# One run of transposes for x and h in the feed-forwards of a three-part transformer block

## What is computed

```python
def ffn(x, w_gate, w_up, w_down):          # fp4_linear rounds both operands to FP4 in blocks of 16
    gate = fp4_linear(x, w_gate)            # 256 -> 704
    y = fp4_linear(x, w_up)
    return fp4_linear(silu(gate) * y, w_down)   # 704 -> 256
x = L0_attn_x                               # 8 x 1024 x 256, float32
x = x + 0.5 * ffn(layernorm(x), w_gate, w_up, w_down)
x = x + attention(layernorm(x), Wq, Wk, Wv, Wo)     # causal, 16 heads of 16
x = x + 0.5 * ffn(layernorm(x), w_gate, w_up, w_down)
```

## Time and profile before

| | us |
|---|---|
| median of three runs | 2040.65 (2039.77 to 2041.57) |
| the profiled execution | 2039.0 |
| its span, first to last instruction | 2037.1 |
| PE busy | 1973.6 (97%) |
| DVE busy | 1838.5 (90%) |
| ACT busy | 1332.6 (65%) |
| POOL busy | 1082.0 (53%) |

### The profile page before, as it was taken

One profiled execution on the slowest core, in us unless ns is written; L12 is line 12 of the kernel. 1 busy time (PEld: TensorE's weight loads), 2 busy tenths in 40 slices (PEclk: granted clock), 3 DMA queues, 4 the chain that ended last, 5 costly groups with the idle time before them and its releaser, 6 DMA issues. The chain is left out here.

```text
span 2037.1 us, 44334 instructions
## 1 busy us (share of the span) xinstructions
PE 1973.6 (97%) x13254; PEld 1299.4 (64%) x13254; DVE 1838.5 (90%) x4649; ACT 1332.6 (65%) x2324; POOL 1082.0 (53%) x1785
## 2 busy tenths in 40 slices
PE   5999999998999999999999999999988899999999
PEld 3888888887887333333333333333328788888888
DVE  7999999998788899999999999999937899999997
ACT  5445445444887788888888888888894354545453
POOL 5888888885664222221222222222222788888885
PEclk9999999999999999999999999999999999999999
DMA  6000000001876655555555554555335000000000
GB/s 215 16 0 0 0 0 0 0 0 37 268 227 214 135 149 136 135 138 137 139 139 149 144 132 138 138 138 138 109 96 199 6 21 20 16 21 21 15 21 27
DMA packets 134842, 185.03 MB, mean 91 GB/s; under 512 B 24928, under 2 KB 76512, under 8 KB 134368
## 3 DMA queue, kind: packets, MB, share of 16 engines
q1 hardware_dynamic: 132000, 182.11, 31.5%
q10 hardware_dynamic: 2688, 1.05, 0.2%
HBM read 113.90 MB, written 85.98 MB: 98 GB/s over the span
## 5 line engine op out<-in xcount | busy, mean ns | idle before, releaser
L1939 POOL TENSOR_SCALAR_AFFINE_SELECT diag_scores<-diag_scores 128x256 f32<-128x256 f32 (+1 forms) x320 | 148.3, 463 | 674.8 <-ACT diag_scores L1908 666.8
L1404 DVE CUSTOM_DVE_ANT_0 gu_ps<-gu_ps,mask_qk 128x256 f32<-128x256 f32 (+3 forms) x690 | 340.5, 529 | 49.7 <-PE gu_ps L1389 42.2
L1389 PE MATMUL gu_ps<-k_stack,q_stack 96*128 96x512 bf16 (+3 forms) x1050 | 318.0, 335 | 2.7 <-DVE part_max L1409 0.5
L1843 PE MATMUL gu_ps<-probs,v_group 128*17 128x512 f32 (+3 forms) x3072 | 310.8, 492 | 3.2 <-ACT probs L1914 2.0
L935 PE MATMUL gu_ps<-wguT_hi,ffn_xT_hi 128*128 128x512 f32 (+1 forms) x768 | 309.1, 402 | 1.2 <-DVE ffn_xT_lo L704 1.2
L935 PE MATMUL gu_ps<-wguT_hi,ffn_xT_lo 128*128 128x512 f32 (+1 forms) x768 | 287.6, 374 | 0.0
L935 PE MATMUL gu_ps<-wguT_lo,ffn_xT_hi 128*128 128x512 f32 (+1 forms) x768 | 287.3, 374 | 0.0
L1910 ACT ACTIVATE probs<-hT_ps 128x256 f32<-128x256 f32 (+2 forms) x320 | 259.7, 811 | 15.0 <-PE hT_ps L1819 14.7
L919 ACT ACTIVATE ffn_z<-xs,ffn_shift,ffn_rstd 128x256 f32 (+1 forms) x128 | 77.0, 602 | 293.2 <-POOL ffn_shift L786 293.2
L1910 ACT ACTIVATE probs<-av_ps 128x256 f32<-128x256 f32 (+2 forms) x320 | 263.6, 824 | 0.3
L1389 PEld LDWEIGHTS gu_ps<-k_stack,q_stack 96*128 96x128 bf16 x1050 | 95.4, 97 | 256.0 <-DVE part_max L1404 183.5
(11 more groups left out here) (221 smaller groups left out, 4893.0 us busy)
## 6 DMA issues: line engine op xcount, KB each, us to landing
q_stack<-q_parts SPq DMA_DIRECT2D x192, 128.0 KB, 3.4
k_stack<-k_parts SPq DMA_DIRECT2D x192, 128.0 KB, 3.6
o_all<-o_sb SPq DMA_DIRECT2D x64, 256.0 KB
q_parts<-qkv_parts SPq DMA_DIRECT2D x32, 384.0 KB, 2.8
k_parts<-qkv_parts SPq DMA_DIRECT2D x32, 384.0 KB, 4.3
v_ones<-qkv_vst SPq DMA_DIRECT2D x16, 544.0 KB, 3.9
v_group<-v_ones SPq DMA_DIRECT2D x32, 272.0 KB, 4.3
xs<-in_L_attn_x SPq DMA_DIRECT2D x8, 1024.0 KB, 8.1
```

The lines of the kernel that those rows point to most:

```text
L1389: mm = T.matmul(out[:, e, :], qs[0:STACK, h0 + e, t * P:(t + 1) * P], ks[0:STACK, h0 + e, c * CHUNK:c * CHUNK + w], start=True, stop=True)
L1404: last = V.tensor_tensor_reduce(out=ps[:, e * w:(e + 1) * w], in0=ps[:, e * w:(e + 1) * w], in1=mask_qk[:, CHUNK - w:CHUNK], scale=1.0, sc ...
L1843: mm = T.matmul(o_ps[h * VPAD:h * VPAD + VCOLS, CHUNK - w:CHUNK], vs[:, t, h, :], probs[:, h // 2, i % 2, h % 2, at:at + w], start=first, ...
L1939: G.affine_select(out=block_of, in_=block_of, compare_op=ALU.is_ge, fill=MASKED, base=0, pattern=[[0, 2], [0, count], [1, P]], channel_mul ...
```

## The change

x and h are transposed in one run into the two banks of hT_ps (six blocks of hq(i-2), then two of xq(i+2)), cast by one instruction and differenced by one, for tiles from 5 on (`ALONE`). The x of tile i+4 travels with the h of tile i (`APART`). Tiles 0 to 4 go alone as before. The parts lie in one tile `turned` with two buffers, h in its first 768 columns, x in the last 256. Waits on xT, xT_hi, xT_lo become, through `x_done`, waits on hT, hT_hi, hT_lo of the tile four earlier. The difference now stands where h's stood, at the head of VectorE's step. VectorE's test of stats and shift moves ahead of g_z (L762).

```diff
+        APART, ALONE = 4, 5
-                xT = [tmp(f"xT_{part}", [P, 2, KD * P], F32R) for part in ("hi", "lo")]
-                hT = [tmp(f"hT_{part}", [P, KH * P], F32R) for part in ("hi", "lo")]
-                hT_end = [tmp(f"hT_end_{part}", [P, KH * P], F32R) for part in ("hi", "lo")]
+                turned = [tmp(f"turned_{part}", [P, 2, (KH + KD) * P], F32R) for part in ("hi", "lo")]
+                xT = [t[:, :, KH * P:(KH + KD) * P] for t in turned]
+                hT = [t[:, :, 0:KH * P] for t in turned]
...
+                def joined(i):
+                    return ok(i) and not (isinstance(i, int) and i < ALONE)
+                def x_done(eng, name, i):
+                    if isinstance(i, int) and min(i, TILES - 1) < ALONE:
+                        if phase * ALONE + i + 1 > 0:
+                            eng.wait_ge(s["xT" + name], phase * ALONE + i + 1)
+                    else:
+                        done(eng, "hT" + name, (min(i, TILES - 1) if isinstance(i, int) else i) - APART)
...
+                        def turned_low(i, par, cols, of):
                             done(dve, "hT_hi", i)
-                            done(dve, "down", i - 1)
-                            V.tensor_tensor(to[1][:], of, to[0][:].bitcast(F32), ALU.subtract).then_inc(s["hT_lo"], 1)
+                            done(dve, "down", i - 2)
+                            V.tensor_tensor(turned[1][:, par, cols], of, turned[0][:, par, cols].bitcast(F32),
+                                            ALU.subtract).then_inc(s["hT_lo"], 1)
...
                             if ok(i - 3) and not early(i - 1, 2):
-                                hT_low(i - 3, hT, hT_flat)
+                                if joined(i + 1):
+                                    turned_low(i - 3, 1 - par, slice(0, (KH + KD) * P), turned_ps)
+                                else:
+                                    hT_low(i - 3, 1 - par, hT_flat)
...
+                            if ok(i + 6):
+                                done(dve, "stats", i + 6)
+                                done(dve, "shift", i + 5)
                             if ok(i + 3):
                                 done(dve, "u_z", i + 3)
...
-                            if ok(i + 6):
-                                done(dve, "stats", i + 6)
-                                done(dve, "shift", i + 5)
-                            if ok(i + 2) and not (early(i, -2) and i == -2):
+                            if ok(i + 2) and not joined(i + 2) and not (early(i, -2) and i == -2):
                                 xT_low(i + 2, par)
...
-                                done(pool, "xT", i + 1)
+                                x_done(pool, "", i + 1)
...
-                        def hT_high(i):
-                            done(act, "down", i - 1)
-                            done(act, "hT_lo", i - 1)
+                        def turned_high(i, par, cols, of):
+                            done(act, "down", i - 2)
                             done(act, "hT", i)
-                            S.copy(hT[0][:], hT_flat).then_inc(s["hT_hi"], 1)
+                            S.copy(turned[0][:, par, cols], of).then_inc(s["hT_hi"], 1)
...
                             if ok(i - 2) and not early(i, 2):
-                                hT_high(i - 2)
+                                if joined(i + 2):
+                                    done(act, "up", i)
+                                    turned_high(i - 2, par, slice(0, (KH + KD) * P), turned_ps)
...
                         def turn_h(i, to):
                             done(pe, "hq", i)
-                            for k in range(KH):
+                            if joined(i + APART):
+                                done(pe, "xq", i + APART)
+                            for k in range(KH + KD if joined(i + APART) else KH):
...
-                            if ok(i + 1):
+                            if ok(i + 1) and not joined(i + 1):
                                 done(pe, "resid", i - 4)
-                                done(pe, "xT_lo", i)
+                                x_done(pe, "_lo", i)
                                 done(pe, "xq", i + 1)
                                 for k in range(KD):
...
-                                done(pe, "xT_hi", i + 1)
-                                done(pe, "xT_lo", i + 1)
+                                if not joined(i + 1):
+                                    x_done(pe, "_lo", i + 1)
```

More of the change, by code:

```diff
@@ L611, in feed_forward @@
                 av_h, av_z = av_flat[:, 0:HIDDEN], av_flat[:, HIDDEN:HIDDEN + DIM]
-                hT_flat = hT_ps[:, :, :].rearrange("p a c -> p (a c)")[:, 0:KH * P]
+                turned_ps = hT_ps[:, :, :].rearrange("p a c -> p (a c)")
+                hT_flat = turned_ps[:, 0:KH * P]
+                assert (KH + KD) * P == 2 * CHUNK
                 hT_end_ps = av_flat[:, 0:KH * P]
@@ L690, in finish @@
                             residual(TILES - 3, down_ps)
-                            hT_low(TILES - 2, hT, hT_flat)
+                            hT_low(TILES - 2, (TILES - 2) % 2, hT_flat)
                             if end:
                                 end["vector"](dve, "low")
-                            done(dve, "hT_hi", TILES - 1)
-                            V.tensor_tensor(hT_end[1][:], hT_end_ps, hT_end[0][:].bitcast(F32),
-                                            ALU.subtract).then_inc(s["hT_lo"], 1)
+                            hT_low(TILES - 1, (TILES - 1) % 2, hT_end_ps)
                             residual(TILES - 2, down_ps)
@@ L702, in xT_low @@
                         def xT_low(i, par):
-                            done(dve, "xT_hi", i)
+                            x_done(dve, "_hi", i)
                             V.tensor_tensor(xT[1][:, par, :], xT_ps, xT[0][:, par, :].bitcast(F32),
@@ L924, in step @@
                             if ok(i - 2) and not early(i, 2):
-                                hT_high(i - 2)
+                                if joined(i + 2):
+                                    done(act, "up", i)
+                                    turned_high(i - 2, par, slice(0, (KH + KD) * P), turned_ps)
+                                else:
+                                    hT_high(i - 2, par, hT_flat)
                         steps("scalar", act, step, finish)
@@ L937, in up_project, with down_project @@
                             return last
-                        def down_project(of, to):
+                        def down_project(of, buf, to):
                             for k in range(KH - 1):
                                 for n, (x, w) in enumerate(passes(of, wdT)):
-                                    T.matmul(to, x[:, k * P:(k + 1) * P], w[:, k, :], start=k == 0 and n == 0, stop=False)
-                            T.matmul(to, of[0][:, (KH - 1) * P:KH * P], wdT_last[:, :], start=False, stop=False)
-                            T.matmul(to, of[1][:, (KH - 1) * P:KH * P], wdT_last_hi[:, :], start=False,
+                                    T.matmul(to, x[:, buf, k * P:(k + 1) * P], w[:, k, :], start=k == 0 and n == 0, stop=False)
+                            T.matmul(to, of[0][:, buf, (KH - 1) * P:KH * P], wdT_last[:, :], start=False, stop=False)
+                            T.matmul(to, of[1][:, buf, (KH - 1) * P:KH * P], wdT_last_hi[:, :], start=False,
                                      stop=True).then_inc(s["down"], 1)
@@ L949, in turn_h @@
                             done(pe, "hq", i)
-                            for k in range(KH):
-                                last = T.matmul(to[:, k * P:(k + 1) * P], hq[:, k * P:(k + 1) * P], ident[:],
+                            if joined(i + APART):
+                                done(pe, "xq", i + APART)
+                            for k in range(KH + KD if joined(i + APART) else KH):
+                                of = hq[:, k * P:(k + 1) * P] if k < KH else xq[:, (k - KH) * P:(k - KH + 1) * P]
+                                last = T.matmul(to[:, k * P:(k + 1) * P], of, ident[:],
                                                 is_transpose=True, start=k % 4 == 0, stop=True, skip_group_check=True)
@@ L970, in finish @@
                             done(pe, "hT_lo", TILES - 2)
-                            down_project(hT, down_ps)
+                            down_project(hT, (TILES - 2) % 2, down_ps)
                             done(pe, "hT_lo", TILES - 1)
-                            down_project(hT_end, down_end_ps)
+                            down_project(hT, (TILES - 1) % 2, down_end_ps)
                         def step(i, par):
                             if ok(i):
-                                done(pe, "xT_lo", i)
+                                x_done(pe, "_lo", i)
                                 done(pe, "silu", i - 1)
                                 up_project(0, par)
-                            if ok(i + 1):
```

(3 more changed lines are left out.)

26 lines of the change are left out of this document (14 added, 12 removed).

## The result

The changed kernel takes 2027.49 us (median of four runs, 2026.65 to 2029.75), the kernel before 2040.49 (2039.77 to 2041.57): a ratio of 0.9938, 95% interval 0.992 to 0.9955, 13.0 us less. The profiled execution took 2027.56 us with a span of 2025.8; against the profiled execution of before (2039.0, span 2037.1) that is 11.4 us less, and 11.3 in span. The forecast was 2028.6, with 12.0 us less.

A forecast was written before the change was run, and what follows sets the result against it. It took ScalarE's order of two casts to bound the 6.81 us step, TensorE a close second. Step 6.815 to 6.71 saves 0.105 × 114 = 12.0 us: 2040.65 − 12.0 = 2028.6 us, range 2025.4 to 2035.5.

The forecast's parts named there:

- closed chain through the two casts: Loop step before: h's cast queues behind x's on ScalarE, whose transposes come 1.47 us later; chain sums to 6.81 us.
- TensorE's floor: Step time that TensorE's work alone would allow in both feed-forwards' loops: 6.81 − 0.12 = 6.69 us.
- exposed 0.12: At the first two down-projection matmuls: late low part of h exposes the weight load, costing 0.12 us a step.
- Transposes: On TensorE, joining runs of six and two into eight: 0.88 us against 0.66 plus 0.23, no gain or loss.
- Cast and difference: ScalarE's joint cast would take 1.03 us and VectorE's joint difference 1.23 us.
- two-step chain: After the change, from VectorE's silu-up product through h's low part and TensorE: 13.38 us for two steps, 6.69 each.
- New wait: Joined run waits for GpSimd's xq half a step earlier: 0.36 us in hand, 0.11 of it signal.
- half-gain rival: Low part or xq stays just late, losing TensorE's 0.12: gain 5 to 9 us, 2032 to 2035.5; chance 0.17.
- slower rival's decision point, e = 0.2: Rival: TensorE waits for xq, late by e; step 6.75 + e/2, so 6.85 us at e = 0.2; chance 0.05.
- same three terms: Sizes assumed for a late xq: 0.27 us delay, 0.11 signal from GpSimd, 0.12 exposed weight load.
- Edges: Steps outside the 114 loop steps hold the same instructions; allowed 1 us either way.
- clock rival: Runs of eight transposes lower TensorE's granted clock: step near 7.53, 81 us slower, 2121; chance 0.01.

The follow-up runs named there:

- e1: Kernel before with one edit: ScalarE's cast of h(i-2) issued ahead of the cast of x(i+2), nothing merged; 2033.47 us, ratio 0.997 to the kernel before.
- e3: Kernel after with the joint cast made to wait until TensorE finishes bank 0 of the next step's up-projection, all merges kept; 2067.97 us.
- e8: Kernel after with output stores held back until the last residual of the second feed-forward is made; 2054.13 us, steps 6.68 and 6.72 us.
- e10: Kernel after with 32 unused bytes a row allocated ahead of `turned` in the second feed-forward alone; 2027.28 us, steps 6.67 and 6.72 us.
- e5: Kernel after with xq issued behind eps on GpSimd instead of ahead of it, no work added; 2033.66 us, steps 6.71 and 6.72 us.
- e6: Kernel after with two of a tile's 17 down-projection matmuls left out, so the result differs; 2019.67 us, steps 6.64 us.
- e4: Kernel after with step 3's 16 filler matmuls moved ahead of the wait for x(4)'s low part, into hT_ps; 2023.03 us, ratio 0.9919 to before.
- e9: e4 with the joined run of transposes waiting for xq only in front of its two x blocks; 2024.07 us.
- e11: e9 with the 32 bytes of padding of e10; 2024.54 us.

## Why the prediction was right, and where not

- *The bound.* The closed chain through the two casts was right: e1 takes it away by order alone, e3 brings it back with all merges kept.
- *TensorE's floor* was put at 6.69 for both; 6.675 and 6.725 were measured, one under and one over, and the two errors nearly cancel. The exposed 0.12 is gone as said. Where the two differ is not settled (e8, e10).
- *Transposes.* Eight take 0.79 to the next L961, as 0.57 + 0.22 said.
- *Cast and difference.* Forecast 1.03 and 1.23 us, measured 0.99 and 1.19: VectorE's way is 6.17 and not 6.23, so the two-step chain is 6.66, not 6.69. Both errors were small and on the safe side.
- *New wait.* The margin was put at 0.25, then 0.13, beyond a signal of 0.11. In the first feed-forward the load starts 0.10 behind xq in the middle step, closer than 0.11 and at the very value that the prediction named as a sign of being wrong. It was no such sign, because a wait for GpSimd that holds the load leaves only 0.05 (e5, e6): xq just arrives in time. Why the margin shrank by more than the step did was not taken apart. The half-gain rival stood closer than thought, yet its price was put too high: e5 costs 0.04 a step. The slower rival's decision point, e = 0.2, was too early by the same three terms.
- *Edges.* "1 us either way" missed the clock: 1.4 us were lost where the fillers run, and 0.75 between the feed-forwards. The loops' 13.3 us in place of 12.0 made up for most of it. That the sum came within 1 us is in part luck: between the two profiled executions the gain is 11.4 us, between the medians 13.0, and the forecast lies between.
- *The clock rival* did not come: 1.00 in both stretches with runs of eight. The half clock that the rows show in after stands elsewhere, at 665.6 and 1556.5 us outside the loops and behind idle time at the fillers, not at a run of transposes in a loop. The Trainium skill, "TensorE: Matmul & The Clock Gate", Part 4 ("PE-mode transpose"), holds that transposes do not count as activity for the clock. Runs of eight, 0.79 us in steps of 6.7, cost no clock here; no run shows a longer one.

## What to carry to other kernels

Where an engine's instruction starts 0.03 us behind another engine's end in every step, follow that engine's queue backwards: the work that it waits for may have been ready long ago, behind a neighbour that was not. Exchanging two instructions on one engine is the cheap test, and here it alone brought half of the gain; look then at what the exchanged neighbour now holds up. Then count the next chains, over two steps as well: here three lay within 0.1 us, which is where the gain ended. Filler matmuls belong into the idle time ahead of a wait, not behind it.

## What the runs showed of the hardware

- A wait met late in front of a weight load costs 0.12 us on the down-projection (gaps 0.23 and 0.19 for 0.18 and 0.12) and up to 0.06 on a run of transposes (0.85 for 0.79, e5).
- A weight load that was held started 0.11 us after VectorE's end (before, e1) and 0.05 after GpSimd's (e5, e6).
- 32 bytes of shift of the loaded operand moved six 512-column matmuls from 1.40 to 1.365 us and the down-projection from 1.87 to 1.91 (e10).
- The same 2.46 us of idle time before the fillers left the clock at 1.00 in one kernel and was followed by 0.50 in the other, where the fillers took 3.56 us in place of 2.15. Placed in the idle time, they took 2.06 to 2.08 in all six rows (e4, e9, e11).
